# Second attention of a Flamingo-like block: output projection as three fp32r passes, context normalised in place, two buffers of probabilities

## Chip, cores and metric

One core of one Trainium2 chip runs the whole program. The metric is the device time of one execution in microseconds (us). The kernel before was timed in three runs.

## The reference, cut to what matters

Two layers, each an attention and a feed-forward part, on x of 8 batches x 256 tokens x 256 features. The change lies in the second layer's attention, where the queries come from a twice normalised x and the keys from the normalised context and that x, 512 keys in all. It has 8 heads of width 128:

```python
    x = x + jnp.tanh(g_xattn[0]) * _L0_xattn_ref(_layernorm(x, axis=-1), ctx_1024, ...)
    x = x + jnp.tanh(g_ffn[0]) * _L0_ffn_ref(_layernorm(x, axis=-1), ...)
    x = x + jnp.tanh(g_xattn[1]) * _L1_xattn_ref(ctx_1024, _layernorm(x, axis=-1), ...)
    x = x + jnp.tanh(g_ffn[1]) * _L1_ffn_ref(_layernorm(x, axis=-1), ...)
```

Per batch and head h the attention computes q, k and v, softmax(q k^T) v, adds the bias of v, and multiplies the result (256 tokens x 128) with the head's 128 x 256 piece of Wo; the eight products are summed.

## The kernel before

The program is a row of four stages with a barrier between them: `attention0`, `slots0`, `attention1` (the change is in it) and `ffn1`. Each stage writes out one instruction list per engine; order on an engine is the order of the list, and semaphores join the engines. Nothing is planned at run time.

`attention1` works in units: one unit is one tile of 128 queries of one head, so a head has two units and a batch 16 (u = 0 to 15). `by_twos` runs batch 0, a loop over batches 1 to 6, and batch 7. Almost all matrix products are split by hand: a value is cast to fp32r (`_hi`), the remainder is kept as a second fp32r tile (`_lo`), and three passes hi*hi, hi*lo, lo*hi are summed (`PASSES`). ScalarE (ACT) makes the `_hi` part out of PSUM, VectorE (DVE) the `_lo` part right after it. Two products are plain fp32 instead: the transposes (L1635, L1581) and the output projection `c_pX` (L1655).

What each engine does in an even unit u of batch b, in order:

- TensorE (PE), L1660: `scores` of unit u+2 (c_pS, three passes of 512 columns), `project_k` (c_pK, six of 512), `turn_probs` of unit u+1 (c_pT), `project_q` (c_pQ, six of 256), `out_project` of the head before (c_pX).
- ACT, L1320: `out_turned` (c_pO plus bias to c_oT, L1318), `turned` (c_pT_hi), `kv_affine` in u = 6 and 8, `exps` of u+2 (c_probs), `k_high`, `q_high`.
- DVE, L1523: `unit_max` of u+2 (c_neg_max), `turned_low` (c_pT_lo), `others` (preparation of the next batch: in u = 0 four bn_stats, in 2 four normalisations, in 4 two), `kv_parts` in 6 and 8, `divide` of u+2 (c_r_sum, c_probs), `k_low`, `q_low`.

In an odd unit PE does `scores`, `project_v` (into c_pK, after a wait for `c_k_lo`, since k_low reads that bank), `turn_probs`, `values` (c_pO, twelve passes of 256) and, in u = 5 and 7, `turn_kv`. DVE does unit_max, turned_low, divide, v_low, and then `others`, which finishes the batch before (odd u). A pair below is an even unit with the odd one behind it. In batch 0 `others` also scales and quantizes the weights of the last stage (u = 9 to 14).

Before the first batch there is a prologue in which the first keys, queries and values are made. SyncE (SP) there issues eight small loads, then Wo (L1241), four loads of the last stage's weights (L1245, L1246), and then the context of each next batch (L1230).

Of the kernel before, what the change touches and what calls it, by code (L numbers as in the profile page):

```python
# [24 lines left out]
ALU = mybir.AluOpType  # L25
# [1127 lines left out]
def attention1(nc, a, x_sb, ident, g_x, w_hi, w_lo, ctx_in, xn3, amax, ffn_w, ffn_scales, ffn_w8):  # L1153
# [9 lines left out]
    with ctx:  # L1163
# [4 lines left out]
        wo = sb("c_wo", [P, H1, D])  # L1168
# [19 lines left out]
        kvn = sb("c_kvn", [P, KT, D])  # L1188
# [12 lines left out]
        probs = sb("c_probs", [P, 4, KEYS])  # L1201
        pT_hi = sb("c_pT_hi", [P, 2, KT, T], F32R)
        pT_lo = sb("c_pT_lo", [P, 2, KT, T], F32R)
        oT = sb("c_oT", [P, 2, T])
# [10 lines left out]
                   kv_lo k k_hi k_lo q q_hi q_lo v v_hi v_lo S max exp rsum probs T T_hi T_lo O oT_sb X ob res stats_o  # L1215
# [7 lines left out]
        def _(sp):  # L1223
# [17 lines left out]
            sp.dma_start(wo[:, :, :], a["L1_xattn_Wo"].rearrange("(h p) n -> p h n", p=P)).then_inc(s["wo"], DMA)  # L1241
# [32 lines left out]
        def _(act):  # L1274
# [69 lines left out]
            kv_affine(0, 1, pK)  # L1344
            act.wait_ge(s["bq"], 1)
# [12 lines left out]
        def _(dve):  # L1358
# [16 lines left out]
            def ctx_normed(n):  # L1375
                dve.wait_ge(s["rstd"], n + 1)
                wait(dve, s["kv"], DC * n)
                for t in range(TT):
                    last = nc.vector.tensor_scalar(kvn[:, t, :], ctx_in[:, t, :], moments[:, t, 0:1], rstd[:, t:t + 1], ALU.subtract, ALU.mult)
                last.then_inc(s["ctxn"], 1)  # L1380
                for t in range(TT):
                    last = nc.vector.tensor_scalar(kvn[:, TT + t, :], x_sb[:, bass.ds(TT * n + t, 1), :].rearrange("p a d -> p (a d)"),
                                                   moments[:, TT + t, 0:1], rstd[:, TT + t:TT + t + 1], ALU.subtract, ALU.mult)
                last.then_inc(s["lat"], 1)

            def lat_stats(n):
# [37 lines left out]

            def unit_max(n, u):
# [3 lines left out]
            def divide(n, u):  # L1429
# [4 lines left out]
                nc.vector.tensor_scalar(probs[:, u % 4, :], probs[:, u % 4, :], r_sum[:, u % 4:u % 4 + 1], None, ALU.mult).then_inc(s["probs"], 1)  # L1434
# [22 lines left out]
            def out_bias(m):  # L1457
                dve.wait_ge(s["X"], m + 1)
# [64 lines left out]
            def batch(b, par, first, last):  # L1523
                for u in range(U1):
# [3 lines left out]
                    turned_low(n, u)  # L1528
                    if u % 2 == 0:
# [23 lines left out]
            kv_parts(0, 0, 1)  # L1553
            for h in range(2):
# [10 lines left out]
            by_twos(dve, batch)  # L1565
            for u in range(1, 14):
# [3 lines left out]
        def _(pe):  # L1570
# [4 lines left out]
            def turn_kv(n, c, bank=pQ):  # L1575
# [4 lines left out]
                for t in range(KT):  # L1580
                    last = nc.tensor.transpose(bank[:, t * P:(t + 1) * P], kvn[:, t, c * P:(c + 1) * P], ident[:, :])  # L1581
# [49 lines left out]
            def turn_probs(n, u):  # L1631
                pe.wait_ge(s["probs"], n + 1)
                wait(pe, s["T_lo"], n - 1)
                for t in range(KT):
                    last = nc.tensor.transpose(pT[:, u % 2, t * P:(t + 1) * P], probs[:, u % 4, t * P:(t + 1) * P], ident[:, :])  # L1635
                last.then_inc(s["T"], 1)

            def values(b, h):
# [3 lines left out]
                wait(pe, s["oT_sb"], H1 * b + h)  # L1642
# [63 lines left out]
            pe.wait_ge(s["wo"], DMA)  # L1706
# [392 lines left out]
```

## Time and profile before

| what | value |
|---|---|
| median of 3 runs | 1053.5 us (1052.11 to 1053.91) |
| span of the profiled execution | 1050.3 us |
| runs' median less that span (what lies around it) | 3.2 us |
| busy over the whole span | PE 876.5, PE weight load 702.4, DVE 754.4, ACT 561.8, POOL 87.9 us |
| first and last record of c_pX | 456.3 and 964.5 us |
| records of c_pX | 256, two for each of 128 matmuls |
| SP: Wo issued, landing after | 419.49 us, 7.2 us |
| SP: first of four loads of the last stage's weights, context of batch 1 issued, its landing after | 419.97 us, 425.32 us, 6.3 us |
| DVE: first bn_stats of the context of batch 1 | 447.11 us |

The page has no time of the profiled execution of its own beside the span; the difference to the runs' median stands in its place. Busy times are per engine and overlap. Matmul records are longer than the distance between their starts, since matmuls are pipelined; distances between starts are the cost of a stream of them. DVE and ACT records overlap their neighbours by some 0.09 us in the same way.

### The profile page before, as it was taken

What the parts mean: (1) busy time and instruction counts of PE and PEld (TensorE: products, weight loads), DVE (VectorE), ACT (ScalarE), POOL (GpSimd) and SP (SyncE); (2) the same over time, 40 slices, a digit from 0 to 9 for tenths busy, and PEclk for the clock granted to TensorE, in tenths of its full rate; (3) what the DMA queues carried; (4) which work ended last, traced back from release to release, by engine and by line L of the source; (5) the groups of instructions that cost most, each with busy time, mean ns of one, the idle gap of its engine ahead of it and who ended that gap; (6) DMA issues with size and microseconds to landing.
All of it is one profiled execution on the core that took longest, in us unless ns stands there. A gap on an engine that the chain in (4) does not pass through costs nothing. (4 is left out here: it accounts for less than half of the span.)

```text
span 1050.3 us, 17086 instructions
## 1 busy us (share of the span) xinstructions
PE 876.5 (83%) x5499; PEld 702.4 (67%) x5499; DVE 754.4 (72%) x1679; ACT 561.8 (53%) x1216; POOL 87.9 (8%) x99
## 2 busy tenths in 40 slices
PE   4468877888865575699999999999999999996666
PEld 4346656666543344588888888888888888885323
DVE  4456766677655585488887888878888788775677
ACT  1356665676633241365555565655656556553665
POOL 2001110111001300000000000000000000000141
PEclk9689988998897687799999999999999999999697
DMA  5485334542203000300000000000000000000102
GB/s 163 79 191 99 68 51 85 100 95 61 35 26 146 1 0 2 110 12 1 9 3 2 11 2 10 0 0 10 0 10 0 0 0 0 1 1 1 28 0 81
DMA packets 37314, 39.15 MB, mean 37 GB/s; under 512 B 7890, under 2 KB 34580, under 8 KB 35476
## 3 DMA queue, kind: packets, MB, share of 16 engines
q1 hardware_dynamic: 37268, 38.57, 15.9%
q8 instruction: 25, 0.41, 0.2%
q14 instruction: 21, 0.17, 0.1%
HBM read 30.17 MB, written 8.39 MB: 37 GB/s over the span
## 5 line engine op out<-in xcount | busy, mean ns | idle before, releaser
L1305 ACT ACTIVATE c_probs<-c_pS,c_neg_max 128x512 f32<-128x512 f32 x128 | 88.0, 688 | 111.6 <-DVE c_neg_max L1427 111.5
L294 ACT ACTIVATE a_probs<-a_pS,a_neg_max 128x256 f32<-128x256 f32 x256 | 105.5, 483 | 72.5 <-DVE a_neg_max L426 71.6
L1427 DVE TENSOR_REDUCE c_neg_max<-c_pS 128x1 f32<-128x512 f32 x128 | 88.2, 689 | 59.1 <-PE c_pS L1628 57.1
L426 DVE TENSOR_REDUCE a_neg_max<-a_pS 128x2 f32<-128x512 f32 x128 | 86.2, 682 | 39.4 <-PE a_pS L581 39.1
L581 PE MATMUL a_pS<-a_k_stack,a_q_stack 96*128 96x256 bf16 x256 | 54.5, 299 | 44.7 <-DMA a_q_stack<-q_parts_dram 44.7
L591 PE MATMUL a_pT<-ident,a_probs 128*128 128x128 f32 x512 | 87.8, 299 | 3.3 <-ACT a_probs L294 3.2
L1422 DVE TENSOR_TENSOR c_pT_lo<-c_pT,c_pT_hi 128x512 fp32r<-128x512 f32 x128 | 87.0, 680 | 1.2 <-ACT c_pT_hi L1313 1.2
L591 PEld LDWEIGHTS a_pT<-ident,a_probs 128*128 128x128 f32 x512 | 65.1, 154 | 24.2 <-issue 17.0
L1645 PE MATMUL c_pO<-c_pT_hi,c_v_hi 128*128 128x256 f32 x256 | 77.5, 303 | 3.1 <-DVE c_pT_lo L1422 3.1
L1635 PE MATMUL c_pT<-ident,c_probs 128*128 128x128 f32 x512 | 76.7, 272 | 0.3 <-DVE c_probs L1434 0.3
L1635 PEld LDWEIGHTS c_pT<-ident,c_probs 128*128 128x128 f32 x512 | 63.5, 140 | 17.8 <-DVE c_probs L1434 0.7
L1318 ACT ACTIVATE c_oT<-c_pO,c_bv 128x256 f32<-128x256 f32 x64 | 30.3, 474 | 83.8 <-PE c_pO L1645 83.8
L1313 ACT CAST c_pT_hi<-c_pT 128x512 fp32r<-128x512 f32 x128 | 74.0, 579 | 0.0
L1645 PE MATMUL c_pO<-c_pT_hi,c_v_lo 128*128 128x256 f32 x256 | 72.0, 281 | 0.0
L1645 PE MATMUL c_pO<-c_pT_lo,c_v_hi 128*128 128x256 f32 x256 | 71.9, 281 | 0.0
L432 DVE COPY a_probsT<-a_pT 128x512 f32<-128x512 f32 x64 | 43.8, 685 | 34.9 <-PE a_pT L591 34.9
L1655 PE MATMUL c_pX<-c_wo,c_oT 128*128 128x256 f32 x256 | 65.9, 380 | 0.7 <-ACT c_oT L1318 0.6
L1434 DVE TENSOR_SCALAR c_probs<-c_probs,c_r_sum 128x512 f32<-128x512 f32 x128 | 62.3, 487 | 4.5
L1628 PE MATMUL c_pS<-c_k_hi,c_q_hi 128*128 128x512 f32 x128 | 63.3, 494 | 0.0
L581 PEld LDWEIGHTS a_pS<-a_k_stack,a_q_stack 96*128 96x128 bf16 x256 | 26.7, 107 | 49.1 <-DMA a_q_stack<-q_parts_dram 26.6
L1591 PE MATMUL c_pK<-c_kv_hi,w_hi 128*128 128x512 f32 x128 | 51.6, 403 | 4.5 <-DVE c_kv_lo L1402 3.9
L301 ACT COPY a_probsT<-a_pT 128x512 f32<-128x512 f32 x64 | 38.1, 595 | 26.4 <-PE a_pT L591 25.9
(309 smaller groups left out, 2267.9 us busy)
## 6 DMA issues: line engine op xcount, KB each, us to landing
a_q_stack<-q_parts_dram SPq DMA_DIRECT2D x48, 128.0 KB, 7.1
k_parts_dram<-a_k_parts SPq DMA_DIRECT2D x8, 384.0 KB, 2.7
q_parts_dram<-a_q_parts SPq DMA_DIRECT2D x8, 384.0 KB, 3.1
a_k_stack<-k_parts_dram SPq DMA_DIRECT2D x8, 384.0 KB, 5.3
a_ctx_in<-in_ctx_dram SPq DMA_DIRECT2D x8, 256.0 KB, 7.5
a_k_stack<-k_parts_dram SPq DMA_DIRECT2D x8, 256.0 KB, 6.3
b_raw<-in_L_xattn_Wkv_dram SPq DMA_DIRECT2D x1, 2048.0 KB, 12.5
ctx_in<-in_ctx_dram SPq DMA_DIRECT2D x8, 256.0 KB, 2.6
```

What stands on the lines that cost most here:

```text
L294: last = nc.scalar.activation(probs[:, u % 4, j, :], pS[:, slot(par, u), j, :], ACT.Exp, bias=neg_max[:, u % 4, j:j + 1])
L426: nc.vector.tensor_reduce(neg_max[:, u % 4, :], pS[:, slot(par, u), :, :], AX_X, ALU.max, negate=True).then_inc(s["max"], 1)
L581: last = nc.tensor.matmul(pS[:, slot(par, u), j, :], q_stack[:, par, h, (u % 2) * P:(u % 2 + 1) * P], k_stack[:, par, h, :], start=True, s ...
L591: last = nc.tensor.transpose(pT[:, u % 2, m * P:(m + 1) * P], probs[:, u % 4, j, k * P:(k + 1) * P], ident[:, :])
L1305: nc.scalar.activation(probs[:, u % 4, :], pS[:, u % 2, :], ACT.Exp, bias=neg_max[:, u % 4:u % 4 + 1], accum_out=sums[:, u % 4:u % 4 + 1]) ...
L1313: nc.scalar.copy(pT_hi[:, u // 2 % 2, :, half], pT[:, u % 2, :].rearrange("p (t q) -> p t q", q=P)).then_inc(s["T_hi"], 1)
L1422: nc.vector.tensor_tensor(pT_lo[:, u // 2 % 2, :, half], pT[:, u % 2, :].rearrange("p (t q) -> p t q", q=P), pT_hi[:, u // 2 % 2, :, half] ...
L1427: nc.vector.tensor_reduce(neg_max[:, u % 4:u % 4 + 1], pS[:, u % 2, :], AX_X, ALU.max, negate=True).then_inc(s["max"], 1)
L1628: last = nc.tensor.matmul(pS[:, u % 2, :], (q_hi, q_lo)[x][:, slot, qs], (k_hi, k_lo)[y][:, slot, :], start=(i == 0), stop=(i == 2))
L1635: last = nc.tensor.transpose(pT[:, u % 2, t * P:(t + 1) * P], probs[:, u % 4, t * P:(t + 1) * P], ident[:, :])
L1645: last = nc.tensor.matmul(pO[:, 0:T], (v_hi, v_lo)[x][:, h // 4, t, (h % 4) * DH:(h % 4 + 1) * DH], (pT_hi, pT_lo)[y][:, h % 2, t, :], sta ...
L1655: last = nc.tensor.matmul(pX[:, t, :], oT[:, h % 2, t * P:(t + 1) * P], wo[:, h, :], start=(h == 0 and t == 0), stop=(h == H1 - 1), skip_g ...
```

## The change

- `out_project`: two fp32 matmuls of 256 columns become six fp32r ones; operands are `c_oT_hi`, `c_oT_lo` and `c_wo_hi`, `c_wo_lo`. It waits for `oT_lo` instead of `oT_sb`, and signals `X` per head instead of per batch.
- A new DVE instruction per head, `out_low`, makes `c_oT_lo` from c_pO, the bias and `c_oT_hi`. It stands in even units behind `turned_low` and ahead of `others`; c_oT now has one buffer, so `out_turned` also waits for `X`.
- Wo is loaded in two pieces into the space of the last stage's raw weights, cast by ACT in the prologue (after the second `kv_affine`), and its remainder made by DVE (after `kv_parts`). SP waits for that before it loads the last stage's weights, and with them the context of batch 1, which is behind them in its list.
- The context is normalised in place in `ctx_in`; its next load waits for the transposes (`kv`), not for the normalisation (`ctxn`). The latents have a tile of their own, `c_latn`.
- `c_probs` has two buffers instead of four; `exps` waits for the transposes of two units back.

```diff
-        wo = sb("c_wo", [P, H1, D])
+        wo_lo = sb("c_wo_lo", [P, H1, D], F32R)
+        wo_hi = sb("c_wo_hi", [P, H1, D], F32R)
...
+        wo_raw = ((ffn_w[0][:, :, :], slice(0, 6)), (ffn_w[1][:, 0:2, :], slice(6, H1)))
...
-                pause(sp, s["ctxn"], n, s["passed_sp"])
+                pause(sp, s["kv"], DC * n, s["passed_sp"])
...
+            for raw, heads in wo_raw:
+                sp.dma_start(raw, wo_view[:, heads, :]).then_inc(s["wo"], DMA)
...
+            sp.wait_ge(s["wo_lo"], 2)
...
-                wait(act, s["T"], n - 3)
+                wait(act, s["T"], n - 1)
...
                 act.wait_ge(s["O"], g + 1)
-                nc.scalar.activation(oT[:, h % 2, :], pO[:, 0:T], ACT.Identity, bias=bv[:, h:h + 1]).then_inc(s["oT_sb"], 1)
+                wait(act, s["X"], g)
+                nc.scalar.activation(oT_hi[:, :], pO[:, 0:T], ACT.Identity, bias=bv[:, h:h + 1]).then_inc(s["oT_hi"], 1)
...
             kv_affine(0, 1, pK)
+            act.wait_ge(s["wo"], 2 * DMA)
+            for raw, heads in wo_raw:
+                nc.scalar.copy(wo_hi[:, heads, :], raw).then_inc(s["wo_hi"], 1)
...
+            def out_low(g, h):
+                dve.wait_ge(s["oT_hi"], g + 1)
+                nc.vector.scalar_tensor_tensor(out=oT_lo[:, :], in0=pO[:, 0:T], scalar=bv[:, h:h + 1], in1=oT_hi[:, :].bitcast(F32),
+                                               op0=ALU.add, op1=ALU.subtract).then_inc(s["oT_lo"], 1)
...
                     turned_low(n, u)
+                    if u % 2 == 0 and (not first or u > 0):
+                        out_low(H1 * b + u // 2 - 1, (u // 2 - 1) % H1)
                     if u % 2 == 0:
                         others(b, u, first, last)
...
             kv_parts(0, 0, 1)
+            dve.wait_ge(s["wo_hi"], 2)
+            for raw, heads in wo_raw:
+                nc.vector.tensor_tensor(wo_lo[:, heads, :], raw, wo_hi[:, heads, :].bitcast(F32), ALU.subtract).then_inc(s["wo_lo"], 1)
...
-                wait(pe, s["oT_sb"], H1 * b + h)
+                wait(pe, s["oT_lo"], H1 * b + h)
...
-                pe.wait_ge(s["oT_sb"], H1 * b + h + 1)
+                pe.wait_ge(s["oT_lo"], H1 * b + h + 1)
...
                 for t in range(TT):
-                    last = nc.tensor.matmul(pX[:, t, :], oT[:, h % 2, t * P:(t + 1) * P], wo[:, h, :], start=(h == 0 and t == 0), stop=(h == H1 - 1),
-                                            skip_group_check=True)
-                if h == H1 - 1:
-                    last.then_inc(s["X"], 1)
+                    for i, (x, y) in enumerate(PASSES):
+                        last = nc.tensor.matmul(pX[:, t, :], (oT_hi, oT_lo)[x][:, t * P:(t + 1) * P], (wo_hi, wo_lo)[y][:, h, :],
+                                                start=(h == 0 and t == 0 and i == 0), stop=(h == H1 - 1 and i == 2), skip_group_check=True)
+                last.then_inc(s["X"], 1)
```

## Rows read from the trace of the kernel before

**Rows 1.** The windows view: busy us of each engine, mean granted clock of TensorE.

```profile
core 0: us, PE busy (x) PEld busy (x) DVE busy (x) ACT busy (x) POOL busy (x), PEclk, DMA share, GB/s
640.00:720.00 80.00, 80.00 (x482) 69.69 (x481) 66.65 (x154) 46.40 (x102) 3.40 (x4) 1.00 0.01 3
```

**Rows 2.** The waits view, 440 to 990 us: total us, times, longest.

```profile
DVE c_neg_max L1427 <- PE c_pS L1628: 57.1, 80, 1.6
...
PEld c_pK L1615 <- DVE c_k_lo L1406: 6.0, 16, 1.2
```

**Rows 3.** The timeline of PE in batch 3: start, duration, idle before in brackets.

```profile
642.08 0.28 PE L1645 MATMUL c_pO<-c_pT_hi,c_v_hi 128*128 128x256 f32 x1
...
643.03 0.28 PE L1645 MATMUL c_pO<-c_pT_hi,c_v_lo 128*128 128x256 f32 x1
...
646.40 1.03 PE L1655 MATMUL c_pX<-c_wo,c_oT 128*128 128x256 f32 x4
...
647.49 0.39 PE L1628 MATMUL c_pS<-c_k_lo,c_q_hi 128*128 128x512 f32 x1
647.72 0.40 PE L1628 MATMUL c_pS<-c_k_hi,c_q_lo 128*128 128x512 f32 x1
...
648.30 0.40 PE L1615 MATMUL c_pK<-w_hi,c_kv_lo 128*128 128x512 f32 x1
```

**Rows 4.** The timeline of DVE over the same pair, u = 0.

```profile
644.66 0.68 DVE L1422 TENSOR_TENSOR c_pT_lo<-c_pT,c_pT_hi 128x512 fp32r<-128x512 f32 x1
...
646.57 0.15 DVE L1432 RECIPROCAL c_r_sum<-c_sums 128x1 f32<-128x1 f32 x1
...
647.16 0.75 DVE L1406 SCALAR_TENSOR_TENSOR c_k_lo<-c_pK,c_bk,c_k_hi 128x512 fp32r<-128x512 f32 x1
647.82 0.48 DVE L1411 SCALAR_TENSOR_TENSOR c_q_lo<-c_pQ,c_bq,c_q_hi 128x256 fp32r<-128x256 f32 x1
648.21 0.68 DVE L1427 TENSOR_REDUCE c_neg_max<-c_pS 128x1 f32<-128x512 f32 x1
```

**Rows 5.** The timeline of the pair of u = 6.

```profile
671.72 0.74 DVE L1406 SCALAR_TENSOR_TENSOR c_k_lo<-c_pK,c_bk,c_k_hi 128x512 fp32r<-128x512 f32 x1
...
672.75 0.40 PE L1615 MATMUL c_pK<-w_hi,c_kv_hi 128*128 128x512 f32 x1
```

**Rows 6.** The timeline of the pair of u = 4.

```profile
662.80 0.74 DVE L1406 SCALAR_TENSOR_TENSOR c_k_lo<-c_pK,c_bk,c_k_hi 128x512 fp32r<-128x512 f32 x1
...
664.26 0.40 PE L1615 MATMUL c_pK<-w_hi,c_kv_hi 128*128 128x512 f32 x1
```

**Rows 7.** The timeline of the pair of u = 12, where DVE has no others.

```profile
694.09 0.68 DVE L1422 TENSOR_TENSOR c_pT_lo<-c_pT,c_pT_hi 128x512 fp32r<-128x512 f32 x1
...
695.01 0.16 DVE L1432 RECIPROCAL c_r_sum<-c_sums 128x1 f32<-128x1 f32 x1 [0.25 <-ACT c_probs L1305]
```

**Rows 8.** The timeline of the last units of batch 7.

```profile
954.40 1.03 PE L1655 MATMUL c_pX<-c_wo,c_oT 128*128 128x256 f32 x4
954.77 0.68 DVE L1422 TENSOR_TENSOR c_pT_lo<-c_pT,c_pT_hi 128x512 fp32r<-128x512 f32 x1
...
957.63 0.39 PE L1645 MATMUL c_pO<-c_pT_hi,c_v_hi 128*128 128x256 f32 x1 [0.54 <-DVE c_pT_lo L1422]
...
960.35 1.29 DVE L1422 TENSOR_TENSOR c_pT_lo<-c_pT,c_pT_hi 128x512 fp32r<-128x512 f32 x2 [1.25 <-ACT c_pT_hi L1313]
...
963.42 0.47 ACT L1318 ACTIVATE c_oT<-c_pO,c_bv 128x256 f32<-128x256 f32 x1 [2.62 <-PE c_pO L1645]
```

**Rows 9.** The timeline of the prologue.

```profile
431.85 0.69 ACT L1287 ACTIVATE c_k_hi<-c_pK,c_bk 128x512 fp32r<-128x512 f32 x1 [4.33 <-PE c_pK L1591]
...
432.57 0.75 DVE L1406 SCALAR_TENSOR_TENSOR c_k_lo<-c_pK,c_bk,c_k_hi 128x512 fp32r<-128x512 f32 x1 [3.86 <-ACT c_k_hi L1287]
```

**Rows 10.** Groups by line and shape, whole run: busy us, mean ns of one, idle before.

```profile
L1411 DVE SCALAR_TENSOR_TENSOR c_q_lo<-c_pQ,c_bq,c_q_hi 128x256 fp32r<-128x256 f32 x64 | 30.6, 478 | 3.9 <-ACT c_q_hi L1292 3.3
...
L815 ACT CAST w_hi<-b_raw 128x4096 fp32r<-128x4096 f32 x1 | 3.6, 3595 | 0.0
...
L510 DVE TENSOR_TENSOR a_w_lo<-a_w_raw,a_w_hi 128x512 fp32r<-128x512 f32 x1 | 1.0, 977 | 0.0
```

More of the change, by code:

```diff
@@ L1187, in attention1 @@
         rstd_o = sb("c_rstd_o", [P, TT])
-        kvn = sb("c_kvn", [P, KT, D])
+        latn = sb("c_latn", [P, TT, D])
         kvf = sb("c_kvf", [P, KEYS])
@@ L1200, in attention1 @@
         r_sum = sb("c_r_sum", [P, 4])
-        probs = sb("c_probs", [P, 4, KEYS])
+        probs = sb("c_probs", [P, 2, KEYS])
         pT_hi = sb("c_pT_hi", [P, 2, KT, T], F32R)
         pT_lo = sb("c_pT_lo", [P, 2, KT, T], F32R)
-        oT = sb("c_oT", [P, 2, T])
+        oT_hi = sb("c_oT_hi", [P, T], F32R)
+        oT_lo = sb("c_oT_lo", [P, T], F32R)
         ob = sb("c_ob", [P, TT, D])
@@ L1302, in exps @@
                 act.wait_ge(s["max"], n + 1)
-                wait(act, s["T"], n - 3)
+                wait(act, s["T"], n - 1)
                 wait(act, s["rsum"], n - 3)
-                nc.scalar.activation(probs[:, u % 4, :], pS[:, u % 2, :], ACT.Exp, bias=neg_max[:, u % 4:u % 4 + 1],
+                nc.scalar.activation(probs[:, u % 2, :], pS[:, u % 2, :], ACT.Exp, bias=neg_max[:, u % 4:u % 4 + 1],
                                      accum_out=sums[:, u % 4:u % 4 + 1]).then_inc(s["exp"], 1)
@@ L1378, in ctx_normed @@
                 for t in range(TT):
-                    last = nc.vector.tensor_scalar(kvn[:, t, :], ctx_in[:, t, :], moments[:, t, 0:1], rstd[:, t:t + 1], ALU.subtract, ALU.mult)
+                    last = nc.vector.tensor_scalar(ctx_in[:, t, :], ctx_in[:, t, :], moments[:, t, 0:1], rstd[:, t:t + 1], ALU.subtract, ALU.mult)
                 last.then_inc(s["ctxn"], 1)
                 for t in range(TT):
-                    last = nc.vector.tensor_scalar(kvn[:, TT + t, :], x_sb[:, bass.ds(TT * n + t, 1), :].rearrange("p a d -> p (a d)"),
+                    last = nc.vector.tensor_scalar(latn[:, t, :], x_sb[:, bass.ds(TT * n + t, 1), :].rearrange("p a d -> p (a d)"),
                                                    moments[:, TT + t, 0:1], rstd[:, TT + t:TT + t + 1], ALU.subtract, ALU.mult)
@@ L1388, in lat_stats @@
                 for t in range(TT):
-                    last = nc.vector.bn_stats(stats_l[:, t, :], kvn[:, TT + t, :])
+                    last = nc.vector.bn_stats(stats_l[:, t, :], latn[:, t, :])
                 last.then_inc(s["stats_l"], 1)
@@ L1394, in lat_normed @@
                 for t in range(TT):
-                    last = nc.vector.tensor_scalar(kvn[:, TT + t, :], kvn[:, TT + t, :], moments_l[:, t, 0:1], rstd_l[:, t:t + 1], ALU.subtract, ALU.mult)
+                    last = nc.vector.tensor_scalar(latn[:, t, :], latn[:, t, :], moments_l[:, t, 0:1], rstd_l[:, t:t + 1], ALU.subtract, ALU.mult)
                 last.then_inc(s["latn"], 1)
@@ L1433, in divide @@
                 dve.wait_ge(s["rsum"], n + 1)
-                nc.vector.tensor_scalar(probs[:, u % 4, :], probs[:, u % 4, :], r_sum[:, u % 4:u % 4 + 1], None, ALU.mult).then_inc(s["probs"], 1)
+                nc.vector.tensor_scalar(probs[:, u % 2, :], probs[:, u % 2, :], r_sum[:, u % 4:u % 4 + 1], None, ALU.mult).then_inc(s["probs"], 1)
             def ffn_row_scales(k):
@@ L1565, in _ @@
             by_twos(dve, batch)
+            out_low(H1 * B - 1, H1 - 1)
             for u in range(1, 14):
@@ L1580, in turn_kv @@
                 for t in range(KT):
-                    last = nc.tensor.transpose(bank[:, t * P:(t + 1) * P], kvn[:, t, c * P:(c + 1) * P], ident[:, :])
+                    last = nc.tensor.transpose(bank[:, t * P:(t + 1) * P], (ctx_in if t < TT else latn)[:, t % TT, c * P:(c + 1) * P], ident[:, :])
                 last.then_inc(s["kv"], 1)
@@ L1634, in turn_probs @@
                 for t in range(KT):
-                    last = nc.tensor.transpose(pT[:, u % 2, t * P:(t + 1) * P], probs[:, u % 4, t * P:(t + 1) * P], ident[:, :])
+                    last = nc.tensor.transpose(pT[:, u % 2, t * P:(t + 1) * P], probs[:, u % 2, t * P:(t + 1) * P], ident[:, :])
                 last.then_inc(s["T"], 1)
@@ L1705, in _ @@
             turn_probs(0, 0)
-            pe.wait_ge(s["wo"], DMA)
+            pe.wait_ge(s["wo_lo"], 2)
             by_twos(pe, batch)
```

6 lines of the change are left out of this document (3 added, 3 removed).

## The prediction

> **What bounds the kernel now.** I read the windows view first. In the middle of the second attention TensorE is busy for 80.00 of 80 us at clock 1.00, its weight loads for 69.69, VectorE for 66.65, ScalarE for 46.40 [rows 1]. So PE sets the pace, but DVE is not far behind, and the change takes work from the one and gives work to the other. A busy share does not say whether DVE has room at the place where the new instruction stands, so I went on to the waits view. It has two entries that matter: DVE waits for the scores of PE 80 times, 57.1 us in all, and PE waits for c_k_lo 16 times, 6.0 us in all [rows 2]. The reader is to see a loop: in each even unit DVE starts only when PE's scores are there, runs through its list down to `k_low`, and PE's `project_v` in the odd unit needs the bank that `k_low` reads. In most pairs DVE gets there early; in 16 it is already late. The timelines of single pairs then give the slack of each kind.
>
> **PE's part.** The old projection starts at 646.40. The second record behind it of the next scores is at 647.49, and 512 columns take 0.23 from start to start (647.49 to 647.72), so the scores in truth begin at 647.26: the block costs 0.86 us. The new one has six fp32r passes of 256 columns; the trace has that form in `values`, where eight steps from 642.08 to 643.03 make 0.119 us each, so 0.71 us. The gain is 0.14 us per head [rows 3]. If the first pass behind another form paid some 0.08 more, it would be 0.06; it can't be much below 0.71, since the weight loads of `values` are the same. [...] The row's 119 ns is this kernel's own, and I go by it.
>
> **DVE's part.** `out_low` is a scalar_tensor_tensor of 128x256 with one PSUM source, one SBUF source and fp32r output. `c_q_lo` is exactly that: 478 ns [rows 10], and in a full queue its slot is 0.39 us (647.82 to 648.21) [rows 4]. I take 0.39 with 0.48 as the upper end. Its input c_oT_hi is made while DVE still waits for the scores, so it adds no wait of its own. Queued behind it are others, kv_parts, divide, k_low and q_low.
>
> How much of 0.39 reaches PE depends on the unit. PE's first `project_v` pass begins 0.15 us after k_low ends where it waited for it: k_low ends at 647.91, the second pass is at 648.30, less 0.23 [rows 3, 4]. Four kinds:
>
> - Bound pairs. In u = 0 and 2 of batches 1 to 6 DVE passes from turned_low to k_low without a gap (no bracket in its rows), and PE waits for it already. All of 0.39 is lost, and PE's gain is lost with it, since a faster PE only waits longer. These are 12, and in batch 0 u = 2, 10 and 12 are like them: 15 x 0.39 = +5.9 us. (With batch 0's u = 0, which has no out_low and no projection, they make the 16 waits [rows 2].)
> - Nearly bound pairs. In u = 6 and 8 k_low ends at 672.46 and PE begins at 672.75. After: 672.46 + 0.39 + 0.15 = 673.00, that is 0.25 later. Batches 0 to 6: 14 x 0.25 = +3.5 us [rows 5].
> - Free pairs with others. In u = 4 k_low ends at 663.54, so PE could begin at 664.08; without a wait it would begin at 664.26 - 0.14 = 664.12. The gain stays, by 0.04 us [rows 6]. 7 pairs.
> - Free pairs without. In u = 10, 12, 14 DVE waits for the exponentials: c_pT_lo's slot ends near 694.70 and r_sum starts at 695.01, so 0.31 of the 0.39 is hidden there, and the rest by k_low's slack [rows 7]. 18 pairs in batches 1 to 6; and batch 7, which prepares no next batch, adds u = 0 to 10, 6 pairs.
>
> The last two kinds are 7 + 18 + 6 = 31 pairs: 31 x -0.14 = -4.3 us. Batch 0's u = 14 has three weight tiles quantized in it; gain and loss cancel, 0. Sum of the pairs: 5.9 + 3.5 - 4.3 = +5.1 us. A middle batch alone gets 2 x 0.39 + 2 x 0.25 - 4 x 0.14 = +0.7 us longer.
>
> **The end of batch 7.** In u = 12 PE has no keys or queries left to project, so the projection is due at 954.40, early. Now it waits for out_low, which stands behind c_pT_lo (954.77): it starts at 955.37 and ends at 955.85. Behind the waiting projection on PE are the scores of the last unit. They come 955.9 - 954.4 - 0.14 = 1.36 later, and with them c_neg_max, then c_pT_lo, for which PE waits at 957.63; DVE was busy a moment before that c_neg_max, so I take +1.25 there. Between the last two c_pT_lo (960.35, two in a row) out_low comes in: +0.4, and the projection behind it, which is late for the last values, +0.1. At the very end oT (963.42) is no longer followed by the projection but by out_low and then it: +0.48 + 0.05 - 0.14. Together +2.1 us [rows 8].
>
> **The prologue.** ACT is idle for 4.33 us until 431.85, DVE for 3.86 until 432.57 [rows 9]. Wo lands at 419.49 + 7.2 = 426.7, before ACT becomes free at 427.5. 2048 columns of cast cost half of the 4096 one, 1.8 us, until 429.3: hidden. The subtraction of 2048 columns costs DVE 2.7 us (four c_pT_lo of 0.68) to 3.9 us (four of 977 ns), until 432.1 or 433.2 [rows 7, 10]. DVE is wanted at 432.57: 0 to 0.7 us. I take 0, since the smaller price is of the commoner row. The cover gone, the whole 1.8 + 2.7 would show.
>
> SP now holds the last stage's weights and the context of batch 1 until about 432.1. These four loads took SP 5.35 us (419.97 to 425.32), and the context landed 6.3 after its issue: about 443.8, up to 444.9. DVE asks for it at 447.11 in u = 0 of batch 0. Hidden, with 2.2 us to spare; if it were gone, each us late is a us once. The weights are wanted at u = 9, far later.
>
> **Edits at nothing.** Two probability buffers: `exps` of unit n+2 now waits for the transposes of unit n, but `turned` ahead of it on ACT waits for the same count. The wait for X in `out_turned`: PE's list has that projection ahead of the values that ACT waits for anyway; same for c_oT's single buffer. Context in place: the next context is issued at u = 7 instead of 2 and is wanted at u = 0 of the next batch, nine units of some 4 us later, for a transfer of under 7 us. X per head: out_bias reads the same moment. If one of these did bite, it would do so in the loop, once per batch.
>
> **The sum.** 5.1 + 2.1 + 0 = +7.2 us. Against the profiled execution: 1050.3 to 1057.5 us of span. What lies around it, 3.2 us, stays: 1053.5 + 7.2 = **1060.7 us**.
>
> Its own range: out_low at 0.48 adds 0.09 x 29 = 2.6; the projection gaining only 0.06 adds 31 x 0.08 = 2.5; the prologue 0.7; u = 4 tipping over, 0.8. Down: PE's 0.15 us after k_low nearer to 0.05, 29 x 0.1 = 2.9; the tail overlapping better, 1. So 1057 to 1065.
>
> **Rivals.**
>
> - A, the other side, not slower: DVE's instruction is absorbed and PE's gain shows in every pair. The mechanism is one: k_low is not what PE waits for in u = 0, 2, 6, 8, some PE-side turnaround is, and the place is the wait ahead of project_v. For it: PE reads 80.00 of 80 busy with DVE at 66.65. Against it: 16 waits named for k_low, and DVE's rows without a gap in these units. It decides where k_low's slack exceeds 0.39 + 0.14 us. It gives 60 x -0.14 + 2.1 = -6.3: 1047.2 us. [...] Chance 0.11.
> - B, no difference: the nearly bound pairs keep their place (a slack of 0.4 more than I see) and the rest is as forecast: 5.9 - 45 x 0.14 + 2.1 = +1.7: 1055.2. For it: no wait is shown in them today. Chance 0.09.
> - C, the projection waits in every pair: out_low late for 646.40. Against: in u = 0 c_pT_lo starts at 644.66 and leaves its slot 0.6 later, so out_low ends by 645.75, 0.65 us ahead of 646.40 [rows 3, 4]. It decides from out_low starting that much later than I put it; at 0.2 us late each, 60 x 0.34 on top of the tail would be +20: 1074. Chance 0.05.
> - D, PE gains nothing: fp32r passes with fresh operands cost 0.86 us as before. Then 31 x 0.14 comes back: 1065. Against: c_pO's steps. Chance 0.05.
>
> The forecast has 0.70. About 0.2% (2.1 us) is what can be told from no change. Faster: A, 0.11 plus 0.01. Same: B with the low edge of the forecast, 0.10. Slower 0.78. For 8 in 10 the range goes from B's 1055 to 1065.
>
> **What would show each step.** c_pX: 384 records, starts 0.119 apart. A c_oT_lo group of 64 at about 478 ns. PE waits for c_k_lo in 29 to 30 places instead of 16, some 12 us longer in total. A middle batch 0.7 us longer than before; its u = 10, 12, 14 pairs shorter by 0.14. In u = 12 of batch 7 the projection waits 1.5 us. No wait of DVE for the context of batch 1. It is wrong if the middle batches get shorter, or if c_pX waits for c_oT_lo inside them.

## The result

| | before | after | ratio, 95% interval |
|---|---|---|---|
| median of 4 runs of each, same chip | 1052.8 us (1050.56 to 1053.91) | 1066.18 us (1065.42 to 1066.4) | 1.0128 [1.0104, 1.0151] |
| span of the profiled execution | 1050.3 us | 1063.6 us | |

The change is 13.4 us slower. The forecast was 1060.7 us, range 1055 to 1065: the sign is right, the size is half of what came, and the time lies outside of the range.

Below, "the loop" is the time from the start of the first scores (c_pS, three passes each) to the start of the last unit's, and a unit is the distance between the starts of two following scores. A start is taken, as in the prediction, from the record of the second pass, less 0.23. A batch begins with the scores that TensorE issues in its u = 0; those of the first two units come before it.

| us | before | after |
|---|---|---|
| first scores | 435.71 | 436.02 |
| first scores to batch 0 | 9.22 | 9.23 |
| batch 0 | 67.20 | 68.61 |
| batches 1, 3, 6 | 65.52, 65.55, 65.52 | 66.24, 66.31, 66.27 |
| batches 2, 4, 5 | 65.52, 65.52, 65.55 | 68.54, 68.97, 67.14 |
| batch 7 to the last scores | 49.98 | 50.49 |
| loop | 519.56 | 531.83 |
| last scores to last c_pX | 9.81 | 10.56 |
| last c_pX to the last record of work | 82.64 | 82.65 |

Outside of the batches only the last projections moved, by 0.75. Inside, three batches stand out. The sum without what is special to them is 1.41 (batch 0) + 6 x 0.75 + 0.51 + 0.75 = 7.2 us, the forecast's own sum; the other 5.8 us lie in the ends of batches 2 and 4 and the start of 5 (2.27, 2.70 and 0.87).

The waits view of after, 440 to 990 us, in the columns of [rows 2]:

```profile
DVE c_neg_max L1442 <- PE c_pS L1649: 56.2, 74, 3.8
...
PEld c_pK L1636 <- DVE c_k_lo L1416: 18.9, 30, 1.7
...
PEld c_pX L1677 <- DVE c_oT_lo L1437: 5.2, 4, 2.0
PEld c_pS L1649 <- issue: 4.8, 2, 2.6
PE c_pS L1649 <- issue: 4.5, 2, 2.5
```

The k_low wait went from 16 times, 6.0 us to 30 times, 18.9 us. The two last lines have nothing to answer to in the same view of before: TensorE stands twice before the scores, and waits for nothing that the profile shows. The timeline of PE has the places:

```profile
646.27 0.28 PE L1666 MATMUL c_pO<-c_pT_hi,c_v_lo 128*128 128x256 f32 x1
648.57 0.47 PE L1649 MATMUL c_pS<-c_k_hi,c_q_hi 128*128 128x512 f32 x1 [2.02 <-issue]
...
783.85 0.47 PE L1649 MATMUL c_pS<-c_k_hi,c_q_hi 128*128 128x512 f32 x1 [2.47 <-issue]
...
784.97 0.63 PE L1612 MATMUL c_pK<-c_kv_lo,w_hi 128*128 128x512 f32 x1
785.40 0.63 PE L1612 MATMUL c_pK<-c_kv_hi,w_lo 128*128 128x512 f32 x1
```

The last instruction of a batch is the twelfth pass of `values`; the next is the first scores of the next batch. Both gaps lie between batches 2 and 3, and 4 and 5: at the jump back of `by_twos`' loop, which holds two batches in a turn, and nowhere else. Behind the second the starts of 512 columns are 0.43 apart (784.97 to 785.40) where a stream at clock 1.00 has 0.23 [rows 3]: after standing 2.47 us TensorE ran at a granted clock of 0.50, and u = 0 of batch 5 took 5.51 in place of 3.95. (512 columns in 0.43 us are 1.19 a ns: this is what the expectations call 1.2 GHz.) Behind the first, of 2.02 us, the granted clock stayed at 1.00. The windows view behind the second and the first:

```profile
785.00:788.00 3.00, 3.00 (x11) 2.43 (x10) 2.96 (x9) 1.35 (x3) 0.00 (x0) 0.50 0.00 0
650.00:653.00 3.00, 3.00 (x22) 2.74 (x21) 2.96 (x9) 2.27 (x5) 0.00 (x0) 1.00 0.00 0
```

The page's DMA section counts the instruction queues. Before, then after:

```profile
q8 instruction: 25, 0.41, 0.2%
q14 instruction: 21, 0.17, 0.1%
```

```profile
q8 instruction: 44, 0.72, 0.3%
q14 instruction: 32, 0.26, 0.1%
```

The DMA view of 634 to 900 us, which lies behind the first turn of the loop, has no instruction packet at all before. After it has these:

```profile
q8 instruction: 18, 0.29, 0.5%
q14 instruction: 10, 0.08, 0.1%
```

q8 belongs to PE and q14 to DVE, as the experiments show: placing TensorE's loop alone takes q8 from 44 to 26 packets and leaves q14 at 32 (e1), placing VectorE's too takes q14 to 23 and leaves q8 at 26 (e5). Before, both engines read the loop's instructions in its first turn and read nothing in the other two, so they still held them. After, both read again in each turn. 0.29 MB in 18 packets are 16 KB each, and 0.08 MB in 10 are 8 KB.

The rest of the profile after, against the rows of before. The first projection block in the loop behind the jump, and the pair that pays:

```profile
651.88 0.28 PE L1677 MATMUL c_pX<-c_wo_hi,c_oT_hi 128*128 128x256 f32 x1
...
652.59 0.39 PE L1649 MATMUL c_pS<-c_k_hi,c_q_hi 128*128 128x512 f32 x1
...
653.84 0.50 PE L1636 MATMUL c_pK<-w_hi,c_kv_hi 128*128 128x512 f32 x1 [0.39 <-DVE c_k_lo L1416]
```

```profile
650.15 0.68 DVE L1432 TENSOR_TENSOR c_pT_lo<-c_pT,c_pT_hi 128x512 fp32r<-128x512 f32 x1
650.75 0.48 DVE L1437 SCALAR_TENSOR_TENSOR c_oT_lo<-c_pO,c_bv,c_oT_hi 128x256 fp32r<-128x256 f32 x1
651.14 0.74 DVE L1380 BATCH_NORM_STATS2 c_stats<-ctx_in 128x6 f32<-128x256 f32 x2
...
653.04 0.74 DVE L1416 SCALAR_TENSOR_TENSOR c_k_lo<-c_pK,c_bk,c_k_hi 128x512 fp32r<-128x512 f32 x1
```

The block is 652.59 - 651.88 = 0.71 us long where it was 0.86 [rows 3]; c_oT_lo's slot is 651.14 - 650.75 = 0.39, as c_q_lo's is in [rows 4]. PE's pass begins 0.06 us after c_k_lo's record ends (653.78).

### The profile page after: what moved, and what is told of

The parts are those of the page before. It is cut to its first block and busy times, and to the rows that moved or that the text cites. A ratio compares the mean times of both kernels' runs of the same rounds, so it can differ in the third digit from the quotient of the medians.

```text
span 1063.6 us, 17485 instructions
## 1 busy us (share of the span) xinstructions
PE 874.4 (82%) x5624; PEld 698.8 (66%) x5627; DVE 780.6 (73%) x1745; ACT 565.0 (53%) x1218; POOL 87.9 (8%) x99
## 5 line engine op out<-in xcount | busy, mean ns | idle before, releaser
L1325 ACT ACTIVATE c_oT_hi<-c_pO,c_bv 128x256 fp32r<-128x256 f32 x64 | 30.4, 475 | 84.6 <-PE c_pO L1666 84.6
L1636 PE MATMUL c_pK<-w_hi,c_kv_hi 128*128 128x512 f32 x124 | 52.1, 421 | 9.2 <-DVE c_k_lo L1416 8.0
L1649 PE MATMUL c_pS<-c_k_hi,c_q_hi 128*128 128x512 f32 x128 | 51.7, 404 | 4.5 <-issue 4.5
## 6 DMA issues: line engine op xcount, KB each, us to landing
b_raw<-in_L_xattn_Wkv_dram SPq DMA_DIRECT2D x1, 2048.0 KB, 12.3
```

The costliest lines, as they stand in the source:

```text
L1636: last = nc.tensor.matmul(bank[:, :], KV[y][:, par, c, kt * P:(kt + 1) * P], W[x][:, c, 2 * INNER + half * 512:2 * INNER + (half + 1) * 51 ...
```

## Experiments

```profile
648.10:654.70 6.60, 6.60 (x29) 5.47 (x29) 4.64 (x11) 2.42 (x5) 0.00 (x0) 0.77 0.01 2
654.70:673.00 18.30, 18.30 (x112) 15.91 (x111) 16.59 (x44) 10.37 (x23) 1.70 (x2) 1.00 0.05 14
```

In the loop's first turn q8 brings seven packets in before (509.5 to 626.5 us) and eight in e1 (513.9 to 631.4), and none behind them until 900 us in either; the change and e3 have 18 between 634 and 900 us. e2 leaves the place alone and gives the loop `hint_back_edge=True`, a hint on its jump back.

**e1, e2: TensorE's loop placed, or hinted.**

```diff
 def by_twos(eng, batch, **how):
-    with eng.Fori(0, (B - 2) // 2) as i:
+    with eng.bass.Fori(0, (B - 2) // 2, engines=bass.OrderedEngineSet([eng.engine]), **how) as i:
-            by_twos(pe, batch)
+            by_twos(pe, batch, head_slot=0)          # e1
+            by_twos(pe, batch, hint_back_edge=True)  # e2
```

> The changed kernel, with the first instruction of TensorE's loop over batches 1 to 6 placed at slot 0 of a fetch block of its instructions; nothing else moves. In the trace after, PE stands still by 'issue' for 2.0 and 2.5 us right behind the last unit of batches 2 and 4, where the loop jumps back, and the 16 KB instruction packets go on all through the loop (44 in the run) where before they cease between 626 and 910 us (25). Theory 1 (fetch): the body has grown by some 64 instructions and now reaches one block too far, so the block at its head is no longer held when it jumps back. Placed at a block's start it fits: both stops go, with them the 1.2 GHz stretch behind the second, 5 to 6 us less: about 1060.5 us; 16 KB packets back near 25. Theory 2 (the stops are part of the new work, such as the wait for X or oT_lo where the loop turns): placement does nothing, 1066.

> [...] Theory 1 (fetch): the packets stay as many (about 44), but the stops at the two jumps shrink or go: 1060 to 1063 us. Theory 2: no difference, 1066. [...]

Measured: e1 1064.29 us, ratio 1.0118 [1.0095, 1.0141]; e2 1063.56, 1.0105 [1.0066, 1.0144]. PE's stops at the jumps are gone in both and q8 is back at 26 packets, none of them between 634 and 900 us. For e2 that was not expected: the hint was to leave the packets at about 44, so how it works stays open, and it is no test of theory 1. And less came back than the 5 to 6 us expected of e1: the loops are 529.07 and 528.14 us, 2.8 and 3.7 less than after, and by the medians it can hardly be told from nothing. The waits view of e1, with two lines of its page under it:

```profile
DVE c_neg_max L1443 <- issue: 4.6, 2, 2.4
```

```profile
q8 instruction: 26, 0.43, 0.2%
q14 instruction: 32, 0.26, 0.1%
```

VectorE stops at the same jumps, in u = 0 and 1 of batches 3 and 5 (67.39 and 67.50 us against 66.28 for 1, 2, 4 and 6). In the change this stop lay under TensorE's, in the 3.8 us that c_neg_max waits for c_pS.

**e3: the kernel before, TensorE's loop 200 places into a block.**

```diff
-            by_twos(pe, batch)
+            by_twos(pe, batch, head_slot=200)
```

> The kernel BEFORE, with TensorE's loop put at slot 200 of a fetch block. Its body is shorter than the changed one, but from slot 200 it too reaches into an eighth block. Theory 1 (fetch): both jumps stop PE for some 2 us each with none of the change in the kernel, 4 to 6 us more: 1057 to 1059, and 16 KB packets near 44. Theory 2: 1053, no difference.

Measured: 1061.51 us, 1.009 [1.0064, 1.0115], above the expected 1057 to 1059. The waits view:

```profile
PEld c_pS L1629 <- issue: 4.7, 2, 2.5
PE c_pS L1629 <- issue: 4.3, 2, 2.3
```

q8 has 44 packets, q14 still 21; the loop is 527.16 us, 7.6 more than before, and behind a stop of 2.01 us the scores' starts are 0.43 apart. Not one instruction of the work differs. So placement alone makes the stop. The loss at a jump is more than the stop where the clock falls behind it, as it does at both jumps here (4.29 us of stops, 7.6 of loop). What the change did to cross the border is told less finely: it made the turn longer, from about 1710 records of TensorE to 1772 (weight loads and the sequencer's among them), and it moved the loop's head too, since batch 0 ahead of it grew in the same way. No run separates the two. The rest of the 9.5 us lies ahead of the second attention, whose first record of VectorE starts at 417.44 where it was at 414.97. In the fourteen profiled runs this start goes from 412.7 to 420.0 with the same work ahead of it, so I compare loops from here on.

**e4, e8: no remainder, without and with TensorE's loop placed.**

```diff
-                    if u % 2 == 0 and (not first or u > 0):
-                        out_low(H1 * b + u // 2 - 1, (u // 2 - 1) % H1)
...
-last = nc.tensor.matmul(pX[:, t, :], (oT_hi, oT_lo)[x][:, t * P:(t + 1) * P], ...
+last = nc.tensor.matmul(pX[:, t, :], (oT_hi, oT_hi)[x][:, t * P:(t + 1) * P], ...
```

> The changed kernel without out_low: the third pass of the projection takes c_oT_hi in place of c_oT_lo, and PE waits for c_oT_hi (the remainder of the attention's output is left out of the product). Same instructions on PE, 64 fewer on DVE. Theory A (what I forecast: DVE's 0.39 us reaches PE through k_low in 29 pairs, and the gain of 0.14 us is lost there): the 29 pairs lose their +0.39 or +0.25, nearly bound pairs gain 0.14, and the end of batch 7 is 2.5 us shorter: 5.9 + 3.5 + 2.0 + 2.5 = 14 us less than the changed kernel, 1052 (with the two stops at the loop's jumps still in it). Theory B (the pairs are longer for another reason, such as six passes in place of two on PE): little changes, above 1063.

> The changed kernel without the remainder (left out: the third pass multiplies oT_hi again), as in the run 1053.0, now with TensorE's loop at the start of a block. It is the floor for the version with POOL. Theory F: the two stops of 2.6 us go (5.1 us), nothing replaces them since VectorE's loop has its old length: batches 64.7 us throughout, 1053.0 - 5.4 = 1047 to 1048. Rival (a stop of VectorE lay under TensorE's here too): batches 3 and 5 stay 1.1 us longer, 1050.

Measured: e4 1053.0 us, 1.0011 [0.9993, 1.0028]; e8 1047.47, 0.9941 [0.9916, 0.9965]. e4's middle batches are 64.7, its loop 518.37 us, 13.5 less than after for an expected 14, with two stops of 2.54 and 2.55 us in it (c_pS L1641 <- issue), behind which the granted clock stays at 1.00. c_k_lo's wait is down to 9.9 us. e8 has no instruction packet between 634 and 900 us and a loop of 512.87, 5.5 less than e4. This is what the projection in fp32r is worth when nobody pays for the remainder: 6.7 us of loop.

**e5: both loops placed.**

```diff
-            by_twos(dve, batch)
+            by_twos(dve, batch, head_slot=0)
-            by_twos(pe, batch)
+            by_twos(pe, batch, head_slot=0)
```

> The changed kernel with the loops over the batches of both TensorE and VectorE placed so that each begins at the start of a block of instructions (each engine's alone; no instruction of the work differs). With TensorE's loop alone placed, VectorE's own stops at the jump remained (neg_max behind 'issue' 4.6 us in all, 2 times, batches 3 and 5 at 67.4 and 67.5 us against 66.3 for the others). Theory F (both stops are instruction fetches of a loop that does not fit where it lies): no stop is left, batches 1 to 6 all take 66.3 us, 2.3 us less than with TensorE's placed alone; median 1059 to 1061, 7 to 8 us above the kernel before, which is what the prediction's other terms add up to (7.2). Rival G (VectorE's loop has grown too long for its store wherever it begins, or the stop passes to ScalarE): 4 us of stops remain somewhere and it stays at 1062 to 1064.

Measured: 1062.69 us, 1.0088 [1.0068, 1.0108]. Batches 2 to 6 are 66.26 to 66.31, and no packet of either queue is left between 634 and 900 us. The loop is 527.16, 7.6 above before. The median misses F's 1059 to 1061 and lies in G's 1062 to 1064. Two things fill the difference. Both engines now stop once where they enter the loop (u = 15 of batch 0 4.98 for 4.09, u = 1 of batch 1 4.82 for 4.61; about 1.2 us together), and the stage starts 1.3 us later. The timeline there:

```profile
515.60 0.47 PE L1650 MATMUL c_pS<-c_k_hi,c_q_hi 128*128 128x512 f32 x1 [0.67 <-issue]
...
516.81 0.69 DVE L1443 TENSOR_REDUCE c_neg_max<-c_pS 128x1 f32<-128x512 f32 x1 [2.33 <-PE c_pS L1650]
```

TensorE's 0.67 is the larger part; e1, where VectorE's loop is not placed, has 0.50 and a u = 15 of 4.81. VectorE's maximum begins 1.21 us behind TensorE's record (515.60 to 516.81), in e1 0.97. What a trace can tell of F and G, the stops and packets at the jumps, speaks for F: no stop of that kind is left in batches 2 to 6. G's "wherever it begins" is refuted.

**e6: the remainder alone, on the kernel before.**

```diff
+            def out_low(g, h):
+                dve.wait_ge(s["oT_sb"], g + 1)
+                nc.vector.scalar_tensor_tensor(out=oT_lo[:, :], in0=pO[:, 0:T], scalar=bv[:, h:h + 1], in1=oT[:, h % 2, :],
+                                               op0=ALU.add, op1=ALU.subtract).then_inc(s["oT_lo"], 1)
```

> The kernel before with its plain fp32 projection, and VectorE's new instruction alone added: once per head it takes oT from pO + bv into a tile that nobody reads, at the place where the change has it, and TensorE waits for it where it waits in the change. Left out of the change: fp32r projection, the split weights, the context in place, two buffers of probabilities. VectorE's loop is placed at the start of a block, so that its longer list does not stop at the jump. Theory A (0.39 us of VectorE per head are paid in the pairs that VectorE's k_low bounds, and TensorE's 0.14 per head gained only where it bounds): the bound pairs as in the changed kernel, a batch of the loop at 66.3 + up to 0.3 to 1.1 us (the free pairs do not get TensorE's 0.14, some 0.14 x 4 more per batch), so some 66.9 a batch, 1052 + 11 = 1062 to 1064. Theory D (the fp32r passes themselves are the loss, VectorE's work is nearly free): 1052 to 1055.

Measured: 1067.58 us, 1.0127 [1.0097, 1.0158], above the expected 1062 to 1064; the loop is 532.27, that is +12.7 (expected +11), the start 4.0 us later. A middle batch is 66.9 as expected, but 1.2 us are VectorE's stop of 2.3 us on entering the placed loop (batch 1 68.1). Its pair of u = 0 in batch 3 is 4.09 + 4.44 = 8.53 us, and e5's 3.95 + 4.60 = 8.55: with TensorE 0.14 slower the bound pair is as long. VectorE's chain sets it, not TensorE's.

**e7: the remainder on POOL.** ScalarE reads c_pO a second time into a spare tile.

```diff
+            def out_whole(g, h):                                    # ACT, behind turned
+                nc.scalar.activation(oT[:, :], pO[:, 0:T], ACT.Identity, bias=bv[:, h:h + 1]).then_inc(s["oT"], 1)
+            def out_low(g):                                         # POOL, its list by units
+                pool.wait_ge(s["oT_hi"], g + 1)
+                pool.wait_ge(s["oT"], g + 1)
+                nc.gpsimd.tensor_tensor(oT_lo[:, :], oT[:, :], oT_hi[:, :].bitcast(F32), ALU.subtract).then_inc(s["oT_lo"], 1)
```

> The changed kernel with the remainder taken off VectorE: ScalarE reads pO a second time into a plain fp32 tile (one activation of 128x256 more per head, behind pT_hi, where it stands 0.5 us waiting for neg_max), and POOL subtracts oT_hi from it (tensor_tensor 128x256 on SBUF; POOL's list is written out by units so that its small powers lie between). TensorE's loop begins at the start of a block. Theory A: VectorE's 0.39 us are gone and its loop fits again; TensorE's 0.14 per head stay; batches of the loop at 64.7 us as in the run without the remainder, no stops: 1052 - 6 = 1045 to 1048, faster than both kernels. Rival P (POOL's subtraction takes over 1.5 us, or slows VectorE beside it, or ScalarE's second read moves exp and k_hi): each head waits for c_oT_lo or k_lo by 0.2 to 0.8 us, 66 to 68 us a batch, 1056 to 1070.

Measured: 1053.35 us, 0.9995 [0.9977, 1.0014], above the expected 1045 to 1048. The loop is 516.83, 2.7 less than before, with middle batches of 64.9 (65.5 for 3 and 5, where q14 still reads in each turn). It was given back behind the loop: +1.6 us to the last c_pX, where heads wait for POOL, and 86.33 us behind it in place of 82.64. The last is in the timeline of the stage behind:

```profile
985.94 1.52 DVE L1949 TENSOR_SCALAR e_dcol<-e_ones_row,e_dscale 128x128 f32<-128x128 f32 x2
986.11 1.26 POOL L1837 TENSOR_TENSOR e_h<-e_up,e_silu 128x512 f32<-128x512 f32 x1 [9.73 <-ACT e_up L1873]
987.38 0.74 DVE L1959 SCALAR_TENSOR_TENSOR e_h<-e_pU,e_gu_scale,e_silu 128x512 f32<-128x512 f32 x1
988.15 0.69 DVE L1911 TENSOR_REDUCE e_hmax<-e_h 128x1 f32<-128x512 f32 x1
988.17 0.13 PEld L2042 LDWEIGHTS e_pU<-e_xT,e_wT 128*128 128x128 bf16 x2 [3.38 <-DVE e_h L1959]
```

The second e_dcol ends 0.08 us behind POOL's e_h. TensorE's weight loads stand 3.38 us, its matmuls 2.89, and from 988.2 to 993 its granted clock is 0.50.

**e9, e10: two attempts at the rest of e7.** e9 places VectorE's loop too and gives the last head's remainder to VectorE; e10 also moves the context's normalisation.

```diff
-                    if u % 2 == 0:
+                    if u % 2 == 0 and u != 2:
                         others(b, u, first, last)
...
                         divide(n + 2, u + 2)
+                    if u == 2:
+                        others(b, u, first, last)
```

> The version with the remainder on POOL, with two edits: VectorE's loop too begins at the start of a block, and the remainder of the last head of all is taken by VectorE straight from pO, as in the changed kernel. In the version with POOL alone the loop gained 2.7 us on the kernel before (first scores to last 516.8 against 519.6), and gave it back outside of it: c_pX ended 1.6 us later behind the last scores (11.4 against 9.8), and the stage behind took 86.3 us against 82.6, with e_dcol of VectorE at 1.52 us instead of 0.47 and TensorE at 1.2 GHz after it. Theory F (e_dcol was VectorE fetching instructions, where the longer program put a border): another placement moves it away, 82.5 us behind c_pX; u=0 and u=1 of batches 3 and 5 lose 0.5 us each; the tail gains 0.8. Sum: 1053.4 - 1.1 - 0.8 - 3.8 = 1047 to 1049, 4 to 6 us under the kernel before. Rival S (the 3.8 us come of something that POOL or the spare tile brings): 1051 to 1052.

> As the run beside it, and in unit 2 VectorE normalises the context after it has divided the probabilities, not before. In the version with POOL the first ctx_in of unit 2 takes 0.64 us where it takes 0.41 without POOL's subtraction beside it, and the pair u=2, 3 takes 8.39 us against 8.15. Theory K (VectorE is slowed by POOL only where both work on SBUF alone at the same time; then the 0.23 us reach TensorE through k_low): with ctx_in behind POOL's 0.74 us the pair is 8.15 again, 7 times 0.24 = 1.6 us less than the run beside it. Rival (c_probs, in SBUF as well, comes beside POOL instead and takes the 0.2 us): no difference, the pair stays at 8.39.

Measured: e9 1055.31 us, 1.0016 [1.0, 1.0033]; e10 1056.3, 1.0027 [1.0011, 1.0044]. Both miss, e9 its 1047 to 1049 and e10 its pair of 8.15 us; the loops are 518.03 and 519.16. In e9 the second e_dcol is as late as in e7, so theory F is wrong for that place, and 88.29 us follow the last c_pX; the loop is entered with a stop as in e5 (batches 0 and 1 are 0.5 us longer each than e7's), and q14 still reads in it; the last c_pX comes 12.22 after the last scores. e10 shows its contention as expected: two ctx_in take 0.73 us together, behind POOL's c_oT_lo, where they took 0.96 beside it in e7. But the pair of u = 2 is 3.95 + 4.55, longer than e9's 3.95 + 4.43: ahead of c_r_sum VectorE now waits 0.25 us for the exponentials, with nothing in between to do.

**e11: the change, both loops placed, the remainder ahead of the maximum.**

```diff
+                    if u % 2 == 0 and (not first or u > 0):
+                        out_low(H1 * b + u // 2 - 1, (u // 2 - 1) % H1)
                     if not last or u + 2 < U1:
                         unit_max(n + 2, u + 2)
                     turned_low(n, u)
-                    if u % 2 == 0 and (not first or u > 0):
-                        out_low(H1 * b + u // 2 - 1, (u // 2 - 1) % H1)
```

> The changed kernel with the loops of TensorE and VectorE at the start of a block (1062.7 us), and VectorE's remainder moved one place ahead, before the maximum of the unit instead of behind pT_lo. There VectorE stands idle until 0.9 us into an even unit while oT_hi is done at 0.67. Theory A (what a pair pays is VectorE's time from the scores to k_low, and only what lies in it counts): the remainder ends at 1.15 instead of costing a place of 0.39, the maximum starts 0.2 later than now; each bound pair loses 0.2 us of its 0.39, three to four pairs a batch, 7 batches: 4 to 5 us less, 1058 to 1059. Rival (the maximum's delay passes to exp and the probabilities, and turn_probs of TensorE waits instead): no gain or a loss, 1062 to 1066.

Measured: 1054.84 us, 1.001 [0.9993, 1.0027], 7.9 less than e5, better than the 4 to 5 expected. The loop is 518.37, 8.8 less than e5, though VectorE's stop on entering it is 2.51 us here and costs 1.5 (u = 1 of batch 1 5.98). Its pairs of u = 0 to 8 in batch 3 are 8.45, 8.37, 8.33, 8.36 and 8.01; e5's are 8.55, 8.57, 8.33, 8.76 and 8.38. The timeline of DVE has why:

```profile
643.96 0.48 DVE L1438 SCALAR_TENSOR_TENSOR c_oT_lo<-c_pO,c_bv,c_oT_hi 128x256 fp32r<-128x256 f32 x1 [1.02 <-ACT c_oT_hi L1326]
644.36 0.68 DVE L1443 TENSOR_REDUCE c_neg_max<-c_pS 128x1 f32<-128x512 f32 x1
```

The same 0.48 us now fills time in which VectorE stood anyway (bracket). In u = 6 and 8 nothing of it is paid (e8, without the remainder, has 8.37 and 8.01), in u = 0 and 2 part (8.18 and 8.14).

**e12: e7, with POOL's first e_h behind e_dcol.**

```diff
+            pool.wait_ge(s["dcol"], 1)
             for n in range(1, FT * NCH, 2):
```

> The version with the remainder on POOL (TensorE's loop at the start of a block, VectorE's where it was; 1053.35 us) with one wait more in the stage behind: POOL's first e_h waits until VectorE has written e_dcol. In that version POOL's e_h (1.26 us, on SBUF alone) began between the two e_dcol, and the second of them took 1.32 us where the first took 0.28; VectorE's first e_h came 1.2 us late, TensorE stood 3.4 us for it, then ran at 1.2 GHz (matmuls of 1.06 us in place of 0.6), and the stretch behind c_pX took 86.3 us in place of 82.6. Theory K (a tensor_scalar of VectorE whose operands are all in SBUF is held while POOL works on SBUF): both e_dcol take 0.28 us, POOL's e_h starts 0.2 us later, TensorE's clock stays up, the stretch is 82.5 us again; median 1053.35 - 3.7 = 1049 to 1050.5, 2.5 to 4 us under the kernel before. Rival F (VectorE was fetching instructions there): the second e_dcol takes over a microsecond still, and the wait adds it to POOL's path: 1053 to 1055.

Measured: 1052.87 us against 1055.31 for before beside it, 0.9974 [0.9955, 0.9992]. Both e_dcol take 0.28 us, and 82.62 us follow the last c_pX: theory K stands. TensorE's granted clock is 0.50 from 988 to 990.5 us all the same, as it is in before from 986 to 988.5. The loop is 517.46. The median is 2.4 us under before, for an expected 2.5 to 4, and the interval of the ratio just leaves out 1: it is faster than before by 0.26%, though not by much more than can be told. The view of the tile e_dcol:

```profile
L1950 DVE TENSOR_SCALAR e_dcol<-e_ones_row,e_dscale x2: 283/283/283, 991.7 to 991.9; 128x128 f32<-128x128 f32 x2
```

## Why the prediction was right in its terms and wrong in its sum

- **The step that failed** is "Edits at nothing": the sum had no term for the loop itself. It says that an edit there, if it bit, "would do so in the loop, once per batch". What bit was none of these edits but the number and the place of the instructions between the loop's head and its jump, once per turn of two batches. It is worth 5.8 us of the 12.3 in the loop: 2.27 and 2.70 for the stops, and 0.87 for the slow clock behind the second. e3 made it in the kernel before by placement alone, e1, e2 and e5 took it away. The rows were there to ask: the page before counts 25 packets on q8, and its DMA view none in the loop's second and third turn (634 to 900 us), so the body was held, with how much room is in no row; and the change adds two matmul records and two weight loads a head to it (c_pX: 256 records before, 384 after). With the stops at the jumps gone (e5) the loop costs 7.6 us and the end behind it 0.75, which is the forecast's 7.2 and 1.2 for the stop on entering.
- **TensorE's part:** right, 0.71 us a block for 0.86, so 0.118 a pass. **VectorE's slot:** right, 0.39.
- **Bound and nearly bound pairs:** right. In batch 3 the pairs of u = 0 and 2 are 0.38 and 0.41 longer; u = 6 0.27 (forecast 0.25) and u = 8 0.34; u = 4 and 10 to 14 are 0.15 to 0.18 shorter. A middle batch: +0.75 for a forecast of +0.7. 30 waits for c_k_lo for 29 to 30, 12.9 us more for some 12.
- **The end of batch 7:** right. 0.51 + 0.75 = 1.26 us, with six pairs of -0.14 in it, so 2.1 for the rest, as forecast. The wait of the projection in u = 12 is 1.33 on PE, for 1.5; its other parts were not set against the rows one by one.
- **The prologue:** right. ACT and DVE still stood 2.45 and 0.78 us ahead of the first c_k_hi and c_k_lo, where it was 4.33 and 3.86 [rows 9]; the first scores came 0.3 us later, with a start of the stage 0.4 later. The subtraction took 1.76 and 0.68 us, less than the 2.7 to 3.9 that it was priced at.
- **Rival A** (VectorE's instruction absorbed) is refuted by e4 and e6 for the place where the change has it, and nearly made true by e11, which puts it where VectorE stands. Relieving TensorE alone, the busiest engine, is worth 6.7 us of loop (e8), but the engine at 66.65 of 80 us [rows 1], which got the work, was on the path in the pairs that pay. **Rival B** is refuted by the 0.27 and 0.34 of u = 6 and 8. **Rival D** is refuted by the block's 0.71. **Rival C** did not occur: c_pX waits for c_oT_lo only in batch 7.
- **The range** was built of the sizes of named steps alone. It had no room for a step that was not named, and the result fell 1.2 us beyond it. Its own terms upward add up to 6.6 us, 1067.3, where it was drawn to 1065; with that end the result would have lain inside by luck, since none of these terms came.

## What to carry to other kernels

Before an edit adds instructions to a long hardware loop, look at the instruction queues in the profile behind the loop's first turn: where they are silent, as here from 634 to 900 us, the body is held, and the sum needs a term for the case that it no longer is (5.8 us here). Afterwards look for waits on "issue" at the jump, on each engine, since the longest hides the others: VectorE's 4.6 us came to light only when TensorE's 4.5 were gone (e1). A new instruction on a nearly full engine cost here by its place in the list more than by its length: the same 0.48 us cost 8.8 us of loop more behind the maximum than ahead of it. And when TensorE stands for 2 to 3 us, look at the granted clock behind it: it was 0.50 behind 2.47 us in the change, and 1.00 behind 2.02.

## What the runs showed of the hardware that was not expected

- TensorE ran the second and third turn of the loop of before without one packet on q8 between 634 and 900 us; with the loop 200 places into a block (e3) it read 18 packets of 16 KB there and stood 2.01 and 2.28 us at the two jumps back. The silent loop of before took seven packets of 16 KB to read in (509.5 to 626.5 us), that of e1 eight (513.9 to 631.4 us), so TensorE holds about 112 KB at least, an estimate from these counts. How much more it has room for no run shows.
- A stop of VectorE of 2.2 to 2.4 us at the jump costs only 1.1 to 1.2 us of TensorE's time (e1); TensorE's of 2.02 and 2.47 cost 2.27 and 2.70.
- The clock does not fall behind every such stop. It was granted at 0.50 behind 2.47 us in the change and behind 2.01 and 2.28 in e3, and stayed at 1.00 behind 2.02 in the change and 2.54 and 2.55 in e4. The length of the stop alone does not decide it; what does is open.
- A placed loop can be entered with a stop: TensorE's of 0.50 us in e1 and 0.67 in e5, VectorE's of 2.3 in e6 and 2.51 in e11; e2, e7 and e8 show none of TensorE. Why is open.
- Two VectorE instructions with all operands in SBUF, both tensor_scalar, are held while POOL works: e_dcol 1.32 us for 0.28, ctx_in 0.96 a pair for 0.73. c_pT_lo, which reads PSUM, was not (in e7 680 ns with and without POOL beside it). What the two engines share there no trace shows. Less than 0.1 us of other timing decided whether it struck: in e7, e9, e10 and e11 POOL's e_h began 0.03 us ahead of the second e_dcol, which took 1.32; in e5 it began 0.07 behind it, e_dcol took 0.28, and e_h 1.34 us instead of 1.26.
